# Two macaron layers on one core: first mixer's products in the order k k v v r r with one reciprocal, second mixer's tables on ACT, expert rows out of PSUM by ACT

## The reference, cut to what matters

```python
# mixer 1, per feature, along the tokens; k, v, r are 128x128 products of shifted mixes of x
p = maximum(pp, u + kk); e1 = exp(pp - p); e2 = exp(u + kk - p)
out = (e1 * aa + e2 * vv) / (e1 * bb + e2)
p2 = maximum(w + pp, kk); e1b = exp(w + pp - p2); e2b = exp(kk - p2)
carry = (e1b * aa + e2b * vv, e1b * bb + e2b, p2)
x = x + (sigmoid(r) * out) @ Wo.T
# mixer 2: retention of 16 heads of 8, with rotary tables cos and sin
q, k = rotate(q), rotate(k)
S = gamma * S + k * v;  o = q . S;  o = groupnorm(o);  x = x + (silu(g) * o) @ Wo.T
```

## Time and profile before

| | us |
|---|---|
| median of 3 runs (781.89 to 784.01) | 782.19 |
| the profiled execution | 787.67 |
| its span | 785.8 |
| PE busy | 616.7 (78%) |
| DVE busy | 450.9 (57%) |
| ACT busy | 330.8 (42%) |
| POOL busy | 404.3 (51%) |
| all indirect scatters on POOL, 184 | 187.2 |
| all indirect gathers on POOL, 184 | 180.6 |
| y copies on DVE, 96 | 39.5 |

### The profile page before, as it was taken

How to read it: one execution, slowest core, us unless ns; L and a number is a source line. 1 busy time by engine, 2 the same in 40 slices (tenths; PEclk the granted TensorE clock), 3 DMA queues, 4 the chain that set the end, 5 groups by cost and what they waited for, 6 DMA issues and landing times. The chain is left out here.

```text
span 785.8 us, 13428 instructions
## 1 busy us (share of the span) xinstructions
PE 616.7 (78%) x4215; PEld 523.0 (67%) x4248; DVE 450.9 (57%) x1251; ACT 330.8 (42%) x580; POOL 404.3 (51%) x434
## 2 busy tenths in 40 slices
PE   1298986886378697898899969999478699997793
PEld 1298986665256687787788867666433269887692
DVE  6736325578866667457254643978779875443002
ACT  2255653467145863464445535231111124553340
POOL 3267775634068524775787877223000275367732
PEclk9999997998579899999999999999679899999997
DMA  9075212200213011431232132000200121114203
GB/s 347 19 247 133 55 48 77 49 14 25 81 41 44 23 46 31 107 80 37 56 94 68 36 104 55 18 15 14 64 0 27 14 51 35 54 43 131 54 26 97
DMA packets 42978, 50.28 MB, mean 64 GB/s; under 512 B 8352, under 2 KB 34336, under 8 KB 42912
## 3 DMA queue, kind: packets, MB, share of 16 engines
q0 software_dynamic: 11776, 24.14, 13.5%
q1 hardware_dynamic: 31136, 25.28, 9.8%
HBM read 32.09 MB, written 17.30 MB: 63 GB/s over the span
## 5 line engine op out<-in xcount | busy, mean ns | idle before, releaser
L1041 POOL DMA_INDIRECT tokens_out<-ys,idx_out x184 | 187.2, 1017 | 170.7 <-DVE ys L1233 127.8
L1031 POOL DMA_INDIRECT xs<-tokens_in,idx_in x184 | 180.6, 982 | 177.6 <-DVE owner L1201 94.1
L586 PE MATMUL bank<-w,hT 128*128 x1288 | 184.9, 287 | 19.9 <-DVE ys L1233 8.7
L586 PEld LDWEIGHTS bank<-w,hT 128*128 128x128 f32 x1288 | 166.2, 198 | 39.6 <-issue 37.8
L785 ACT ACTIVATE w_up<-w 128x728 f32 (+1 forms) x184 | 130.8, 716 | 115.2 <-PE bank L564 83.4
L564 PE MATMUL bank<-xT_kept,w_up 128*128 128x128 f32 x1104 | 157.4, 293 | 23.2 <-ACT gate L803 11.2
L564 PEld LDWEIGHTS bank<-xT_kept,w_up 128*128 128x128 f32 x1104 | 145.2, 207 | 28.4 <-issue 15.8
L1233 DVE COPY ys<-bank 128x256 f32<-128x256 f32 x96 | 39.5, 411 | 140.7 <-PE bank L589 102.2
L806 ACT ACTIVATE hT<-bank 128x512 f32<-128x512 f32 x92 | 54.9, 597 | 153.9 <-PE bank L573 150.6
L573 PEld LDWEIGHTS bank<-xT_kept,w_up 128*128 128x128 f32 x736 | 99.8, 197 | 8.4 <-issue 5.3
L573 PE MATMUL bank<-xT_kept,w_up 128*128 128x128 f32 x736 | 99.5, 279 | 5.5 <-issue 3.7
(11 more groups left out here) (168 smaller groups left out, 702.4 us busy)
## 6 DMA issues: line engine op xcount, KB each, us to landing
yg<-tokens_out SPq DMA_DIRECT2D x64, 128.0 KB, 2.7
w<-in_w SPq DMA_DIRECT2D x8, 536.0 KB, 9.4
tokens_in<-xn SPq DMA_DIRECT2D x16, 256.0 KB, 2.9
w<-in_w SPq DMA_DIRECT2D x8, 512.0 KB
xs<-tokens_in,idx_in POOLq DMA_INDIRECT x184, 2.9
tokens_out<-ys,idx_out POOLq DMA_INDIRECT x184, 2.2
x<-in_x SPq DMA_DIRECT2D x2, 512.0 KB, 8.6
out<-x SPq DMA_DIRECT2D x8, 128.0 KB
```

The costliest lines, as they stand in the source:

```text
L586: last = mm(y, hT[0:n_f, n % 2, c * P:(c + 1) * P], w_of(k, e, WD[k] + c * P, P, n_f), start=(c == 0), stop=(k == 0 and c == CH[k] - 1))
L1031: pool.indirect_dma_start(xs[:, j % RING, :], None, xn_dram[b], tile_rows(idx_in, b, j))\
L1041: pool.indirect_dma_start(ys_dram[b], tile_rows(idx_out, b, j), ys[:, j % RING, :], None)\
```

## The change

1. Mixer 1: PE's order is k0 k1 v0 v1 r0 r1, with bank CB[b] + i for column half i. k1 waits for no other product, v0 for e20 (last reader of k0), v1 for e21, r0 for n20, r1 for n21. ACT's order is exp0, exp1, tanh0, tanh1. `inverse` is gone; DVE takes one `reciprocal` of the denominator and multiplies.
2. `copies_y` goes from DVE to ACT, with the same waits. Expert tiles of kind 1 don't use DVE any more.
3. The tables of mixer 2: the widened rotary table, the centring matrix with its diagonal and the spread weights of v are made by ACT; the two stripe matrices by one DVE reduction each (were 24 POOL instructions); the product of both by DVE at the end of pass 3. POOL keeps the variance matrix.
4. All five strings of turns are new. On SP the write of half 0's rows for pass 2 comes before the `yg` loads of half 1 for pass 1.

```diff
-        RW_PE = [Steps(sem(f"rw_pe{b}"), ["k0", "v0", "r0", "k1", "v1", "r1"]) for b in range(NB)]
+        RW_PE = [Steps(sem(f"rw_pe{b}"), ["k0", "k1", "v0", "v1", "r0", "r1"]) for b in range(NB)]
...
-                        ("k", 0, 0, 0, (RW_DVE, "e20")), ("v", 0, 1, 1, (RW_DVE, "n20")),
-                        ("r", 0, 2, 0, (RW_ACT, "th0")), ("k", 1, 0, 0, (RW_DVE, "e21")),
-                        ("v", 1, 1, 1, (RW_DVE, "n21")), ("r", 1, 2, 0, (RW_ACT, "th1"))):
+                        ("k", 0, 0, (RW_DVE, "e20")), ("k", 1, 0, (RW_DVE, "e21")),
+                        ("v", 0, 1, (RW_DVE, "n20")), ("v", 1, 1, (RW_DVE, "n21")),
+                        ("r", 0, 2, (RW_ACT, "th0")), ("r", 1, 2, (RW_ACT, "th1"))):
...
-                    to = take(CB[b] + own, reader[0][b], 0, reader[1])
+                    to = take(CB[b] + i, reader[0][b], 0, reader[1])
...
+            def retention_tables():
+                act.wait_ge(ld_rope, 16)
+                run(rope_wide, heads(raw, 2 * NCH, DH).unsqueeze(2).to_broadcast([P, 2 * NCH, H, DH]), ACT.Copy, RS_COPY)
...
+            def copies_y():
+                for p in range(len(PASSES)):
+                    for m in range(NPAIR):
+                        yield
+                        n, at = min(2, TILES - 2 * m), 2 * m % RING
+                        act.wait_ge(down_done, p * TILES + 2 * m + n)
+                        if p or 2 * m >= RING:
+                            pair = m % (RING // 2)
+                            act.wait_ge(st_ys[pair], 16 * (p * stored_from(pair) + 2 * (m // (RING // 2))))
+                        nc.scalar.activation(ys[:, at:at + n, :], heads(ybank[:, 0:n * P], n, P), ACT.Copy)\
+                            .then_inc(y_copied, 1)
...
-                def inverse(i):
-                    after(RW_POOL[b], 0, f"den{i}")
-                    after(RW_DVE[b], 0, f"n2{i}")
-                    run(rw_ex[:, i, 3, :], rw_ex[:, i, 1, :], ACT.Ln, RW_INV[b])
-                    after(RW_INV[b], 0, f"ln{i}")
-                    run(rw_ex[:, i, 3, :], rw_ex[:, i, 3, :], ACT.Exp, RW_INV[b], scale=-1.0)
...
-                after(RW_INV[b], 0, f"inv{i}")
-                step(V.tensor_tensor(rec, den, inv, ALU.mult))
-                after(RW_DVE[b], 0, f"dr{i}")
-                step(V.scalar_tensor_tensor(rec, rec, -2.0, inv, ALU.add, ALU.mult))
-                yield
-                after(RW_DVE[b], 0, f"rec{i}")
-                step(V.tensor_tensor(wkv, wkv, rec, ALU.mult))
+                after(RW_POOL[b], 0, f"den{i}")
+                step(V.reciprocal(den, den))
+                after(RW_DVE[b], 0, f"rec{i}")
+                yield
+                step(V.tensor_tensor(wkv, wkv, den, ALU.mult))
...
-            weave(TURNS["dve"], products(), beside(0), beside(1), decay_setup(), copies_y(), key_tables())
+            weave(TURNS["dve"], products(), beside(0), beside(1), decay_setup(), key_tables(), retention_back())
```

More of the change, by code:

```diff
@@ L175, in build_block @@
         gn = sb("gn", [P, 2])
-        scale = sb("scale", [P, 1])
+        scale = sb("scale", [P, 3])
         gam = sb("gam", [P, 4, H])
@@ L328, in build_block @@
                           ("kv", "aa", "bb", "n1", "n2", "num")]
-                       + [f"{s}{i}" for i in range(NH) for s in ("dr", "rec", "wkv", "rwkv")]) for b in range(NB)]
+                       + [f"{s}{i}" for i in range(NH) for s in ("rec", "wkv", "rwkv")]) for b in range(NB)]
         RW_ADD = [Steps(sem(f"rw_add{b}"), [f"x{i}" for i in range(NH)]) for b in range(NB)]
@@ L341, in build_block @@
                        + ["x0", "x1"]) for b in range(NB)]
-        RS_POOL = Steps(sem("rs_pool"), ["wide", "neg", "diag", "v", "vzero", "var", "row16"] + [f"row16_{k}" for k in range(1, NCH)]
-                        + ["row8"] + [f"row8_{h}" for h in range(1, H)] + ["back"])
+        RS_POOL = Steps(sem("rs_pool"), ["vzero", "var"])
+        RS_COPY = Steps(sem("rs_copy"), ["wide", "neg", "diag", "v"])
         RS_PE = Steps(sem("rs_pe"), [f"rope{i}" for i in range(2 * NH)])
         RS_ACT = Steps(sem("rs_act"), [f"rope{i}" for i in range(2 * NH)])
-        RS_DVE = Steps(sem("rs_dve"), ["half", "zero", "power", "base", "mine", "gamma"])
+        RS_DVE = Steps(sem("rs_dve"), ["half", "zero", "power", "base", "mine", "gamma", "row16", "row8"])
+        RS_BACK = Steps(sem("rs_back"), ["neg", "own", "back"])
         block = ctx.enter_context(nc.Block())
@@ L650, in rope_table @@
                     yield
-                    after(RS_POOL, 0, "wide")
+                    after(RS_COPY, 0, "wide")
                     to = take(CB[0] + i % 2, RS_ACT, 0, f"rope{i}")
@@ L667, in retention @@
                         after(NM_ACT[b], 4, f"xnT{NH - 1}")
-                        after(RS_POOL, 0, "back")
+                        after(RS_POOL, 0, "var")
+                        after(RS_COPY, 0, "v")
+                        after(RS_BACK, 0, "back")
                     project(i, sq[:, M_QK:M_QK + P], 0, (RE_DVE, f"t1q{i}"))
@@ L816, in rwkv_weights @@
                     run(rw_w[:, 2 * j + 1, :], w, ACT.Copy, RW_W, scale=rw_v[:, j:j + 1])
+            def retention_tables():
+                same = const[:, K_BLOCK:K_BLOCK + P]
+                own_head = heads(same, H, DH)[:, :, 0]
+                yield
+                act.wait_ge(ld_rope, 16)
+                raw = ret[:, T_RAW:T_RAW + 2 * NCH * DH]
+                run(rope_wide, heads(raw, 2 * NCH, DH).unsqueeze(2).to_broadcast([P, 2 * NCH, H, DH]), ACT.Copy, RS_COPY)
+                yield
+                after(RS_BACK, 0, "own")
+                center = ret[:, T_OUT:T_OUT + DH * P]
+                run(heads(center, DH, P), same.unsqueeze(1).to_broadcast([P, DH, P]), ACT.Copy, RS_COPY, scale=scale[:, 1:2])
+                after(RS_COPY, 0, "neg")
+                diagonal = heads(ret[:, T_OUT:T_OUT + DH * (P + 1)], DH, P + 1)[:, :, 0:P].rearrange(
+                    "p j (h k) -> p j h k", k=DH)[:, :, :, 0]
+                run(diagonal, own_head.unsqueeze(1).to_broadcast([P, DH, H]), ACT.Copy, RS_COPY, scale=scale[:, 2:3])
+                yield
+                run(heads(ret[:, T_V:T_V + DH * P], DH, H, DH),
+                    sq[:, M_V:M_V + P].rearrange("p (h j) -> p j h", j=DH).unsqueeze(3).to_broadcast([P, DH, H, DH]),
+                    ACT.Copy, RS_COPY)
+            def copies_y():
+                for p in range(len(PASSES)):
+                    for m in range(NPAIR):
+                        yield
+                        n, at = min(2, TILES - 2 * m), 2 * m % RING
[5 more added lines that the diff above has]
+                            .then_inc(y_copied, 1)
             def copies_w():
@@ L836, in gate_half @@
                     after(RW_PE[b], 0, f"r{i}")
-                    run(zT[:, b, i * HALF:(i + 1) * HALF], bank[CB[b]][:], ACT.Tanh, RW_ACT[b], scale=0.5)
+                    run(zT[:, b, i * HALF:(i + 1) * HALF], bank[CB[b] + i][:], ACT.Tanh, RW_ACT[b], scale=0.5)
                 def exponents(i):
@@ L1279, in rwkv_exponents @@
                 e1b, e2b, e1, e2 = (rw_ex[:, i, a, :] for a in range(4))
-                k = bank[CB[b]][:]
+                k = bank[CB[b] + i][:]
                 after(RW_SET, 0, "bb0")
@@ L1303, in rwkv_sums @@
                 num = e1b
-                v = bank[CB[b] + 1][:]
+                v = bank[CB[b] + i][:]
                 aa0, aa1, aa_start = rwkv_halves(rw_aa, i)
@@ L1451, in decay_setup, with retention_back, step @@
                 step(V.tensor_reduce(gamma[:, 0:1], power, AX.X, ALU.add), "gamma")
+                eye = const[:, K_ID:K_ID + P]
+                step(V.tensor_reduce(stripes[:, 0:H], eye.rearrange("p (k h) -> p h k", h=H), AX.X, ALU.add), "row16")
+                step(V.tensor_reduce(stripes[:, H:H + NCH], eye.rearrange("p (h k) -> p k h", k=NCH) if False else heads(eye, NCH, H),
+                                     AX.X, ALU.add), "row8")
+            def retention_back():
+                def step(ins):
+                    ins.then_inc(RS_BACK.sem, 1)
+                yield
+                dve.wait_ge(ld_ret, 16 * 3)
+                step(V.tensor_scalar(scale[:, 1:2], scale[:, 0:1], -1.0 / DH, None, ALU.mult))
+                step(V.tensor_scalar(scale[:, 2:3], scale[:, 0:1], 1.0 - 1.0 / DH, None, ALU.mult))
+                yield
+                dve.wait_ge(ld_rope, 16)
+                after(RS_DVE, 0, "row8")
+                step(V.tensor_tensor(heads(ret[:, T_BACK:T_BACK + NCH * P], NCH, H, DH),
+                                     stripes[:, 0:H].unsqueeze(1).unsqueeze(3).to_broadcast([P, NCH, H, DH]),
+                                     stripes[:, H:H + NCH].unsqueeze(2).unsqueeze(3).to_broadcast([P, NCH, H, DH]), ALU.mult))
             def first_norm(b):
```

71 lines of the change are left out of this document (11 added, 60 removed), and 63 rows, old and new, of the table TURNS.

## The result

The changed kernel takes 755.83 us (median of 4 runs, 754.71 to 756.79), the kernel before 783.1 us in the runs beside it: a ratio of 0.964 [0.961, 0.968], faster by 3.6%, and 27.3 us between the medians. The forecast was 762 in a range of 746 to 776. The profiled executions are 787.67 and 756.79 us, their spans 785.8 and 755.0, so 30.8 us have to be found in the traces; 3.5 of them are there only because the profiled execution before lies further above its median (787.67 to 783.1) than the one after (756.79 to 755.83).

The account below looks back on a forecast made before the run. No engine was full throughout; a chain of scatter, mixers, routes, passes 3 and 4, PE in pass 5, then DVE set the end. Span 785.8 - 20 = 765.8, run 767.7, less 5.5 for the median: 762, range 746 to 776.

Parts of the forecast that it names:

- Scatter of pass 0: POOL's last scatter of pass 0 behind 10 gathers instead of 16: half 0's mixer starts 3 us earlier.
- Order and holes: First mixers, order k k v v r r: DVE's two waits go, 4.7 and 6.0 us in half 0, 4.6 and 6.4 in half 1.
- Division: First mixers: reciprocal of 128x512 taken as 3.0 us, between 0.69 and 5.2; division 9.9 us, 0.9 longer than before.
- Route of half 0: Half 0's mixer to pass 2's first gather: one gain and losses of some 3 us, taken as 0.
- Half 1's mixer: Beside pass 2: scan near 228 instead of 229.6; in all 14.2 us gained, so pass 3 starts 14 us earlier.
- more is handed on: Rival: gather 11 not waited for, both halves' 12.8 and 12.6 us add up, some 12 us more, 750; chance 0.20.
- Passes 3 to 5: 14 us kept through passes 3 and 4, 4 gained by POOL gathering pass 5 earlier, 4 lost to idle PE in pass 5.
- End of pass 5: Half 1's adds no longer wait for loads, Newton chain among them: ends at 549.3 where it was 569.4, gain 20 us.
- To the end: From pass 5's end through half 1's retention and pass 7, with nearly the same orders: the gain stays 20 us.
- The slower rival: y copies in ACT's queue hold up the tile loop, 0.45 us each on PE, 43 us less the 20: 805; chance 0.08.
- The signs: Expected in the trace: DVE holes gone, reciprocal near 3 us, four table loads a mixer half, pass 2's first gather at 202 to 210.

Follow-up runs that it names:

- the control: The changed kernel, unedited, timed on a slow chip where the kernel before took 915.3 us: 878.42 us, ratio 0.958.
- two orders mended: Changed kernel with DVE's index steps ahead of half 1's first add and PE's transposes of tiles 8 to 11 behind k1: 751.3 us, ratio 0.9553 (first run 0.951).

## Why the prediction was right, step by step

*The number: right, and nearer than its steps were.* The sum gave 767.7 for the profiled execution, which took 756.79: 10.9 too slow. The forecast then took off 5.5 us, the distance of the profiled run before from its median; the one after stands only 1.0 above its own. So the median is missed by 6.2 (762 for 755.83), and the 4.5 between is luck.

*Scatter of pass 0: mis-sized, and the largest of the terms behind those 10.9 us.* Predicted 3 us at the mixer's start, measured 8.5 (148.29 to 139.77). The add moved by 5.4 us (123.45 to 118.06), close to what the step's own count gives: six gathers (7.6) less a bias part (104.67 to 107.61 on POOL, 2.9) are 4.7. The step then gave back more than half for gathers that come later. The trace shows nothing given back: first add to the norm's last step takes 17.5 us before and after. A further 3.1 us lie behind that step (24.84 to 21.71 from add to scan). Before, a y copy that waited 2.69 us for a scatter and a product that waited 2.58 for PE stood there; now it is a product without a wait. The copy's part in it isn't shown: with the copies back on DVE add to scan was no longer than in the control, on another chip (33.3 and 34.4).

*Order and holes: right.* Predicted 4.7 + 6.0 - 0.9 = 9.8 us for half 0, measured 44.93 - 34.80 = 10.1. Half 1: 4.6 + 6.4 + 2.5 - 0.9 = 12.6 against 47.83 - 35.44 = 12.4. The old order put back into the changed kernel costs 30 us.

*Division: right as a middle.* R was 3.0 and is 3.34 (3343 ns, the mean of four). From the end of the sums to the last gate it takes 10.4 us (164.21 to 174.57) where 9.9 were predicted and 9.0 were before. That the old path would now be 2.1 us longer was not foreseen.

*Route of half 0: right.* Last gate to first gather: 26.1 before, 26.2 after. Of the two losses named there the add was real: with it out of the way (two orders mended) the route takes 24.3, 1.9 less. The five products were not tested.

*Half 1's mixer: right in mechanism.* The scan was put 21.5 us behind the first gather and came 21.7 behind it. It stands at 222.4 and not at 228 through the first step's error. Pass 3 starts 21 us earlier for 14: 5.6 of the difference is that, and 1.3 is the route of half 1, which was to keep its length (32.1 before, 30.8 after). The rival "more is handed on" did not come true by its condition, since gather 11 was waited for: PE's transposes stood 2.00 us for it.
```profile
217.05 0.50 PE L546 MATMUL bank<-const,xs 128*128 128x128 f32 x2 [2.00 <-DMA xs<-tokens_in,idx_in]
```
The time measured, 755.8, lies midway between the forecast and that rival's 750.

*Passes 3 to 5.* Kept + 4 was predicted; the first silu of pass 5 on ACT is 26.6 us earlier (454.24 to 427.64) for 21 at pass 3, so 5.6. POOL's queue is the likely cause: with the tables back on it the first gather of pass 5 came 15.9 us later, but in another slot than in the kernel before, so the 5.6 itself isn't shown. The last state product is 21.2 us earlier; the 4 + 4 that cancel in the prediction cancelled here (21.0 + 5.6 - 5.4).

*End of pass 5.* The adds have no load wait, as the step said. From the last state product to the last gate it counted 16.3 us, 3.6 of them for the Newton chain among the adds; it took 16.7 (22.4 before). The gates end 26.9 us earlier (569.37 to 542.43) for 20: 6.9 more, as much as pass 3 already started early. To the end of the span it is 30.8, where the step "To the end" kept the gain as it was. Most of the last 4 us is gained in pass 7: its first gather is 27.9 us earlier (695.88 to 667.97), its last scatter 31.3 (773.72 to 742.46). The step named two scatters that stand ahead of that pass's last gather and gave nothing for them; whether they are the cause was not tested.

*The slower rival.* PE waits 3.0 us for y copies in all. That its mechanism is real the kernel before with the copies on ACT shows, at ten per cent.

*The signs.* The holes, the reciprocal's row, the four table loads of a mixer and the adds without a load wait came as named, the adds at 525.67 and not in 545 to 560. The first gathers of passes 2 and 3 came before their windows (200.74 for 202 to 210, 288.65 for 292 to 298), by the same mis-sized step.

## What to carry to other kernels

Where each engine runs one fixed order, a removed wait was worth its length at every seam behind it only when the items around it were moved too: the new dependencies in the old turns of DVE lost 1%, and in the new turns the old order costs 30 us. Before moving a DMA issue or a copy between queues, ask what it waits for and what stands behind it; its own duration was the smaller price each time here. Taking one part back out of a tuned schedule prices that schedule without the part, not the part. A stretch nearly free of waits was predicted to a few tenths here: half 0's mixer was to be 9.8 us shorter and was 10.1 shorter, and it took 34.80 to 34.82 us in all six profiles that leave it as changed; half 1's, with waits in it, took 35.44 to 39.37.

## What the runs showed of the hardware

The reciprocal of 128x512 fp32 took 3.34 to 3.35 us on DVE in all 40 instances of the nine profiles that have one (3339 to 3354 ns), 4.8 times the plain product of the same tile behind it (0.69, 692 ns). The same programs ran 16 to 17% slower on two chips than elsewhere (before: 916 and 783 us, changed: 878 and 756), with the large DVE and ACT instructions no longer (reciprocal 3345 and 3343 ns, y copy 379 and 378) and a mean granted clock of 0.893 for 0.932 in the profiles of the changed kernel. Past the first 30 us the changed kernel has 4 stretches of over 1.5 us, 12.5 us in all, in which none of PE, DVE and ACT works; there it has 18, with 46.3. That is 34 of the 113 us by which the two spans differ, and the cause of either is open.
